# Second attention: probabilities stationary in pieces of 32 queries, in four column tiles of the array, and the result turned by VectorE

## The chip, the core and the metric

The kernel runs on one core of a Trainium2 chip. A core has a matrix engine (TensorE, PE in the profile, its weight loads PEld), VectorE (DVE), ScalarE (ACT), GpSimd (POOL) and SyncE (SP), whose queue issues DMA transfers. They run side by side, each in its own written order, and wait for each other by semaphores. The metric is the device time of one execution in microseconds.

## The reference

Two transformer layers in fp32 over x of 32 x 64 rows of 512. Each layer adds a cross-attention to ctx_4096 and then a feed-forward part: layer 0 has attention over features and a top-2 mixture of 8 experts, layer 1 is this, followed by a gated feed-forward of width 1376:

```python
# second attention: 32 query heads in 8 groups of 4, head dimension 16
q = (layernorm(x) @ Wq).reshape(b, s, 8, 4, 16)
k = (ctx @ Wk).reshape(b, s, 8, 16)
v = (ctx @ Wv).reshape(b, s, 8, 16)
scores = einsum('bqhgd,bkhd->bhgqk', q, k) / 4
attn = softmax(scores, axis=-1)
out = einsum('bhgqk,bkhd->bqhgd', attn, v).reshape(b, s, 512)
x = x + out @ Wo
```

## The kernel before

The program has four phases, one after the other: first attention, experts, second attention (`second_attention`, from line 1021) and feed-forward. The change touches the second attention alone.

That phase works through 16 tiles of 128 rows, two batches of 64 queries each. Within a tile the work goes by batch b (0 or 1) and by g (0 or 1), two of the four heads of every group. `scores` (L1411) multiplies in four row tiles of the array (32 rows each), into the four banks of `ps`; VectorE takes the maximum (L1546) and subtracts it (L1553), ScalarE takes the exponential (L1281), `transpose_probs` (L1435) turns the result on TensorE, `keep_probT` (L1287) copies it to `probT`. `attend(t, b, g)` (L1450) then makes 4 products: stationary is a 128 x 128 block of `probT` (the 64 keys of two key heads by 2 members of the group x 64 queries), moving are 34 columns of `kv` (for two heads 16 values and a column of ones, which gives the softmax's sum). An fp32 product that is no transpose stands in the trace as two pairs of weight load and matmul. After both g, `invert_sums` (L1560) and `keep_attn` (L1565) divide by the sums into `attn`, with the queries on the partitions. `transpose_attn` (L1461) turns `attn` of the whole tile on TensorE, four transposes into bank b2; `keep_high_attn` (L1292, ScalarE) and `keep_low_attn` (L1572, VectorE) split that into a rounded part `aT_hi` and the rest `aT_lo`, and `project` (L1376, L1377, L1381, twelve products of 512 columns) multiplies by Wo. `add_attn` (L1577) adds the result to x.

The order on every engine is written out by hand, one round m of a loop at a time. TensorE in round m: scores(m,0), transpose_x(m+1), attend(m-1,1,0), attend(m-1,1,1), make_q(m+1), scores(m,1), transpose_probs(m,0,0) and (m,0,1), transpose_attn(m-1), attend(m,0,0), transpose_q(m+1), attend(m,0,1), project(m-1), transpose_probs(m,1,0) and (m,1,1). transpose_x(m+1) uses the bank of project and waits for add_attn(m-2) (L1370). VectorE in round m begins with add_attn(m-2) and ends with sum_x2(m+3) (L1519), the norm's sums of a tile three rounds ahead, for which it waits until GpSimd has added the experts' rows to it.

Beside this run three other queues. SyncE in round m: load_x1(m+3) (L1106, from m = 3 on: the ring for x holds 6 tiles, so tiles 6 to 15 are loaded here, each after the store of the tile six before it has landed, L1105), load_kv (L1111), load_gate_up(m+1) (L1117, weights of the feed-forward into one of two stage buffers, after low_part two tiles before), store_x3(m-2) (L1121), store_norm(m-2) (L1125). GpSimd in round m: spread_keys(m+1) (L1205), scale_x2(m+2), add_rows(m+3) (L1177 and L1179), scale_x3(m-2), gather(m+5) (L1168, two indirect DMAs), low_part(m-1) (L1213). ScalarE has, besides the copies and exponentials, high_part(m-1) (L1297), which low_part needs, and norm_x and norm_x3.

Of the kernel before, what the change touches and what calls it, by code (L numbers as in the profile page):

```python
# [13 lines left out]
P = 128  # L14
# [1006 lines left out]
def second_attention(nc, shared, a, late):  # L1021
# [3 lines left out]
    with ExitStack() as stack:  # L1025
# [8 lines left out]
        q_rows, qT, attn, n_out = (sb(n, [P, DIM]) for n in ("q_rows", "qT", "attn", "n_out"))  # L1034
# [4 lines left out]
        smax, rsum = sb("smax", [P, 2, 16]), sb("rsum", [P, 2, 2, KVH, 1])  # L1039
# [8 lines left out]
                 "q_rows_kept qt_made s_shifted exp_done pt_made pt_kept o_made sum_step o_kept at_made ahi_kept alo_kept w_made x3_ready")  # L1048
        (zeroed, const_made, proj_hi_made, proj_lo_made, gu_hi, gu_lo, x2_added, x2_ready, stat_step, mv_ready, rs_step,
         rs_ready, xn_ready, xt_made, xhi_kept, xlo_kept, q_made, q_kept, kv_made, kt_kept, v_kept, keys_ready, s_made, max_step,  # L1050
         q_rows_kept, qt_made, s_shifted, exp_done, pt_made, pt_kept, o_made, sum_step, o_kept, at_made, ahi_kept, alo_kept, w_made, x3_ready,
# [192 lines left out]
        def _(act):  # L1244
# [44 lines left out]
            def keep_high_attn(t):  # L1289
                act.wait_ge(at_made, t + 1)  # L1290
                want(act, w_made, t)
                act.activation(aT_hi[:, :].rearrange("p (g b q) -> p b g q", g=GROUP, b=2),  # L1292
                               b2[:, :].rearrange("p (b g q) -> p b g q", b=2, g=GROUP), ACT.Copy).then_inc(ahi_kept, 1)
# [51 lines left out]
        def _(pe):  # L1345
# [68 lines left out]
            def transpose_probs(t, b, g):  # L1414
                n = 4 * t + 2 * b + g
                pe.wait_ge(exp_done, 2 * t + b + 1)
                if b:
                    if g == 0:
                        want(pe, alo_kept, t)
                        if t == 0:  # L1420
                            pe.wait_ge(q_rows_kept, 2)
                    elif t + 1 < TILES:
                        pe.wait_ge(q_kept, t + 2)
                elif g:
                    if t + 1 < TILES:
                        pe.wait_ge(xlo_kept, t + 2)
                    else:
                        pe.wait_ge(x3_ready, t - 1)
                elif t:
                    pe.wait_ge(pt_kept, 4 * t)  # L1430
                else:
                    pe.wait_ge(q_kept, 1)
                for j in range(4):
                    at = 256 * j + P * g
                    mm = pe.transpose(probs_bank(b, g)[:, P * j:P * j + P], score[:, b, at:at + P], ident[:, :])  # L1435
                mm.then_inc(pt_made, 1)

            def attend(t, b, g):
                n = 4 * t + 2 * b + g
                if n == 0:  # L1440
                    pe.wait_ge(values_zeroed, 3)
                    pe.wait_ge(kt_kept, EARLY)
                    pe.wait_ge(v_kept, EARLY)
                if t >= EARLY and b == 0 and g == 0:
                    pe.wait_ge(kv_loaded[t % 4], 16 * ((t - EARLY) // 4 + 1))
                pe.wait_ge(pt_kept, n + 1)
                want(pe, o_kept, 2 * t + b)
                for j in range(4):
                    at = 136 * g + 34 * j
                    mm = pe.matmul(po[:, at:at + 34], probT[:, g, P * j:P * j + P],  # L1450
                                   kv[:, t % EARLY, P + 136 * b + 34 * j:P + 136 * b + 34 * j + 34], start=True, stop=True)
                mm.then_inc(o_made, 1)

            def transpose_attn(t):
                pe.wait_ge(o_kept, 2 * t + 2)
                if t + 2 < TILES:
                    pe.wait_ge(q_rows_kept, t + 3)
                else:
                    pe.wait_ge(pt_kept, 4 * t + 3)
                for i in range(4):  # L1460
                    mm = pe.transpose(b2[:, P * i:P * i + P], attn[:, P * i:P * i + P], ident[:, :])  # L1461
                mm.then_inc(at_made, 1)
# [19 lines left out]
            for m in range(TILES + 1):  # L1482
# [13 lines left out]
                if 0 <= m - 1 < TILES:  # L1496
                    transpose_attn(m - 1)
# [13 lines left out]
        def _(dve):  # L1511
# [43 lines left out]
            def heads():  # L1555
                return po[:, 0:272].rearrange("p (c h d) -> p c h d", c=2, h=KVH)

            def invert_sums(t, b):
                dve.wait_ge(o_made, 4 * t + 2 * b + 2)
                dve.reciprocal(rsum[:, b, :, :, :], heads()[:, :, :, HD:HD + 1]).then_inc(sum_step, 1)  # L1560

            def keep_attn(t, b):
                dve.wait_ge(sum_step, 2 * t + b + 1)
                want(dve, at_made, t)
                dve.tensor_tensor(attn[:, 256 * b:256 * b + 256].rearrange("p (c h d) -> p c h d", c=2, h=KVH), heads()[:, :, :, 0:HD],  # L1565
                                  rsum[:, b, :, :, :].to_broadcast([P, 2, KVH, HD]), ALU.mult).then_inc(o_kept, 1)

            def keep_low_attn(t):
                dve.wait_ge(ahi_kept, t + 1)
                want(dve, w_made, t)  # L1570
                order = "p (g b q) -> p b g q"
                dve.tensor_tensor(aT_lo[:, :].rearrange(order, g=GROUP, b=2), b2[:, :].rearrange("p (b g q) -> p b g q", b=2, g=GROUP),  # L1572
                                  aT_hi[:, :].bitcast(F32).rearrange(order, g=GROUP, b=2), ALU.subtract).then_inc(alo_kept, 1)
# [33 lines left out]
            for m in range(TILES + 2):  # L1607
# [14 lines left out]
                if 0 <= m - 2 < TILES:  # L1622
                    sum_x3(m - 2)
                    average_x3(m - 2)
# [10 lines left out]
                if m + 3 < TILES:  # L1635
                    sum_x2(m + 3)
                    average_x2(m + 3)
# [368 lines left out]
```

## Time and profile before

| | us |
|---|---|
| Median of 3 runs | 975.94 (974.81 to 982.37) |
| The profiled execution | 983.04, its span 981.3 |
| Granted TensorE clock over the span | 0.955 |
| Second attention in the profiled execution | about 335 to 582 |
| TensorE's work between: attends (L1450), 344 to 560 | 60.0 for 470 records of a matmul |
| transpose_attn (L1461), same stretch | 8.4 for 56 |

The profile counts the time that each engine works; idle time of an engine that does not set the pace costs nothing. A view of the timeline gives the start, the duration and, in brackets, how long the engine stood idle before and what ended that. Records of matmuls overlap, so a group's duration is shorter than the sum of its members.

### The profile page before, as it was taken

Reading aid. Unit: us, or ns where it says so; the run is one execution under the profiler, and the core shown is the slowest. Engines: PE = TensorE matmul, PEld = TensorE weight load, DVE = VectorE, ACT = ScalarE, POOL = GpSimd, SP = SyncE. Lnnn points to the kernel's source line nnn. Section 1 sums busy time; section 2 is a strip of 40 time slices with the busy share of each in tenths; the row PEclk is TensorE's granted clock in tenths of the full one; section 3 lists DMA queues with packets and bytes.
Section 4 is the critical chain, followed back from the end, with each engine's and each line's share of the span. In section 5 each row is a group of like instructions: output and inputs, shape, how many; then the busy total and the mean of one; then the engine's idle time right before and its main releaser. Section 6 shows DMA issues by size and latency. Waiting matters only on the chain. (4 is left out here: it accounts for less than half of the span.)

```text
span 981.3 us, 16773 instructions
## 1 busy us (share of the span) xinstructions
PE 916.7 (93%) x6065; PEld 759.9 (77%) x6065; DVE 435.3 (44%) x866; ACT 348.1 (35%) x567; POOL 293.8 (30%) x415
## 2 busy tenths in 40 slices
PE   6999987899998799999999956999999999999997
PEld 4888876788887688888878845888788788878885
DVE  3988865344444556765657621222312122223112
ACT  3556643233332355555546522222111112111111
POOL 4588863000003665565654220111202000202000
PEclk9999998899998879999989976999999999999999
DMA  8566655794544232434422214111003001202001
GB/s 267 172 226 235 198 188 192 267 312 164 161 149 151 66 105 88 149 104 132 134 80 83 83 54 150 43 43 41 1 11 108 12 0 42 66 1 86 1 1 43
DMA packets 56801, 108.20 MB, mean 110 GB/s; under 512 B 8242, under 2 KB 12338, under 8 KB 56594
## 3 DMA queue, kind: packets, MB, share of 16 engines
q1 hardware_dynamic: 49954, 88.13, 27.8%
q0 software_dynamic: 5120, 16.78, 5.2%
q10 hardware_dynamic: 1648, 2.23, 0.6%
q8 instruction: 51, 0.84, 0.3%
q14 instruction: 28, 0.23, 0.1%
HBM read 67.99 MB, written 39.12 MB: 109 GB/s over the span
## 5 line engine op out<-in xcount | busy, mean ns | idle before, releaser
L1900 DVE SCALAR_TENSOR_TENSOR d_hid<-d_pup,d_b_up,d_silu 128x512 f32<-128x512 f32 (+1 forms) x44 | 33.0, 751 | 235.4 <-PE d_pup L1829 235.4
L1790 ACT ACTIVATE d_silu<-d_pgate,d_b_gate 128x512 f32<-128x512 f32 (+1 forms) x44 | 30.3, 689 | 154.7 <-PE d_pgate L1829 154.7
L1761 POOL TENSOR_TENSOR d_x_res<-d_x_res,d_b_down 128x512 f32<-128x512 f32 x16 | 22.0, 1405 | 187.1 <-DMA d_x_res<-x_after_attention 187.1
L1168 POOL DMA_INDIRECT c_y_in<-expert_results,y_at x32 | 32.7, 1023 | 145.6 <-POOLq L98 137.5
L1827 PE MATMUL d_pgate<-d_nT_hi,gate_up_hi 128*128 128x512 f32 (+1 forms) x176 | 71.5, 406 | 1.4 <-DVE d_nT_lo L1889 1.4
L1797 ACT ACTIVATE d_hid_hi<-d_hid 128x512 fp32r<-128x512 f32 (+1 forms) x44 | 27.8, 632 | 125.3 <-DVE d_hid L1900 125.3
L1829 PE MATMUL d_pgate<-d_nT_hi,gate_up_lo 128*128 128x512 f32 (+1 forms) x176 | 70.3, 400 | 0.0
L1828 PE MATMUL d_pgate<-d_nT_lo,gate_up_hi 128*128 128x512 f32 (+1 forms) x176 | 70.0, 397 | 0.0
L1859 PE MATMUL d_pdown<-d_down_hi,d_hid_hi 128*128 128x512 f32 (+1 forms) x176 | 69.5, 395 | 0.0
L1827 PE MATMUL d_pup<-d_nT_hi,gate_up_hi 128*128 128x512 f32 (+1 forms) x176 | 69.5, 395 | 0.0
L1829 PE MATMUL d_pup<-d_nT_hi,gate_up_lo 128*128 128x512 f32 (+1 forms) x176 | 69.3, 394 | 0.0
L1860 PE MATMUL d_pdown<-d_down_lo,d_hid_hi 128*128 128x512 f32 (+1 forms) x176 | 69.3, 393 | 0.0
L1828 PE MATMUL d_pup<-d_nT_lo,gate_up_hi 128*128 128x512 f32 (+1 forms) x176 | 69.1, 392 | 0.0
L1450 PE MATMUL c_po<-c_kv,c_probT 128*128 128x34 f32 x512 | 66.7, 283 | 0.6 <-ACT c_probT L1287 0.6
L1450 PEld LDWEIGHTS c_po<-c_kv,c_probT 128*128 128x128 f32 x512 | 65.0, 203 | 2.0 <-issue 0.5
L1546 DVE TENSOR_REDUCE c_smax<-c_ps 128x16 f32<-128x1024 f32 x32 | 39.1, 1220 | 38.1 <-PE c_ps L1411 38.1
L1012 DVE TENSOR_TENSOR b_biased<-b_py,b_bias 128x512 f32<-128x512 f32 x39 | 27.0, 691 | 63.8 <-PE b_py L972 63.8
L986 ACT ACTIVATE b_rowsT_hi<-b_pt 128x512 fp32r<-128x512 f32 x39 | 23.4, 600 | 86.3 <-PE b_pt L955 86.3
L1908 DVE TENSOR_TENSOR d_hid_lo<-d_hid,d_hid_hi 128x512 fp32r<-128x512 f32 (+1 forms) x44 | 33.9, 770 | 36.5 <-ACT d_hid_hi L1797 36.5
L1865 PE MATMUL d_pdown<-d_down_hi,d_hid_lo 128*128 128x512 f32 (+1 forms) x176 | 47.8, 393 | 0.0
L1287 ACT ACTIVATE c_probT<-c_bank 128x512 f32<-128x512 f32 x64 | 34.9, 595 | 35.0 <-PE c_bank L1435 35.0
L1281 ACT ACTIVATE c_score<-c_score 128x1024 f32<-128x1024 f32 x32 | 33.7, 1054 | 21.7 <-DVE c_score L1553 21.7
(271 smaller groups left out, 2145.8 us busy)
## 6 DMA issues: line engine op xcount, KB each, us to landing
b_rows<-expert_rows SPq DMA_DIRECT2D x39, 256.0 KB, 2.8
expert_results<-b_result SPq DMA_DIRECT2D x39, 256.0 KB, 2.5
a_wstage<-L_ffn_W_e SPq DMA_DIRECT2D x16, 512.0 KB, 4.2
c_stage<-gate_up SPq DMA_DIRECT2D x16, 344.0 KB, 3.2
late_x<-x_after_attention SPq DMA_DIRECT2D x16, 256.0 KB, 3.8
x_after_attention<-late_x SPq DMA_DIRECT2D x16, 256.0 KB, 3.4
norm_after_attention<-c_n_out SPq DMA_DIRECT2D x16, 256.0 KB, 3.3
d_n_in<-norm_after_attention SPq DMA_DIRECT2D x16, 256.0 KB, 2.8
```

What stands on the lines that cost most here:

```text
L1281: act.activation(score[:, b, :], score[:, b, :], ACT.Exp, scale=SCALE1).then_inc(exp_done, 1)
L1287: act.activation(probT[:, g, :], probs_bank(b, g)[:, :], ACT.Copy).then_inc(pt_kept, 1)
L1450: mm = pe.matmul(po[:, at:at + 34], probT[:, g, P * j:P * j + P], kv[:, t % EARLY, P + 136 * b + 34 * j:P + 136 * b + 34 * j + 34], start= ...
L1546: dve.tensor_reduce(smax[:, b, :].rearrange("p (r g) -> p r g", r=4), all_scores(), AX.X, ALU.max).then_inc(max_step, 1)
L1827: pe.matmul(bank[0:w, :], gu_hi[:, cols], nT_hi[:, g % 2, k, :], start=k == 0, stop=False)
L1828: pe.matmul(bank[0:w, :], gu_hi[:, cols], nT_lo[:, g % 2, k, :], start=False, stop=False)
L1829: mm = pe.matmul(bank[0:w, :], gu_lo[:, cols], nT_hi[:, g % 2, k, :], start=False, stop=k == KD - 1)
L1859: pe.matmul(pdown[n][:, :], hi, down_hi[0:w, i, :], start=i == 0, stop=False)
L1860: pe.matmul(pdown[n][:, :], hi, down_lo[0:w, i, :], start=False, stop=False)
L1865: mm = pe.matmul(pdown[n][:, :], lo, down_hi[0:w, i, :], start=False, stop=i == LAST)
L1900: dve.scalar_tensor_tensor(hid[0:w, s % 2, :], pup[s % 2][0:w, :], b_up[0:w, i:i + 1], silu[0:w, s % 2, :], ALU.add, ALU.mult).then_inc(hi ...
L1908: dve.tensor_tensor(hid_lo[0:w, s % 2, :], hid[0:w, s % 2, :], hid_hi[0:w, s % 2, :].bitcast(F32), ALU.subtract).then_inc(lo_made, 1)
```

## The change

`attend` makes its four products of a 128 x 128 block as sixteen: the stationary side is a piece of 32 queries (128 x 32), and the product of pair of heads j goes to column tile j of the array and so to the partitions 32 j to 32 j + 31 of `po`; the moving side is the same 34 columns. The partitions of `po` now stand for the pair of key heads and a place in a piece, and its columns run over g and q (the piece). `invert_sums` and `keep_attn` treat it in that order. The turned tile comes from a block transpose (32 x 32 blocks) on VectorE, `turn_attn`, two a tile, into a new buffer `attnT` in SBUF; `transpose_attn` on TensorE and its use of bank b2 go. `keep_high_attn` and `keep_low_attn` read `attnT`. transpose_probs(m,1,0), which writes b2, waits for q_rows_kept or pt_kept in place of alo_kept. `turn_attn(m-1, 1)` stands on VectorE between sum_x3 and average_x3, `turn_attn(m, 0)` between sum_x2 and average_x2.

```diff
...
                 act.activation(probT[:, g, :], probs_bank(b, g)[:, :], ACT.Copy).then_inc(pt_kept, 1)
 
             def keep_high_attn(t):
-                act.wait_ge(at_made, t + 1)
+                act.wait_ge(a_turned, 2 * t + 2)
                 want(act, w_made, t)
-                act.activation(aT_hi[:, :].rearrange("p (g b q) -> p b g q", g=GROUP, b=2),
-                               b2[:, :].rearrange("p (b g q) -> p b g q", b=2, g=GROUP), ACT.Copy).then_inc(ahi_kept, 1)
+                act.activation(aT_hi[:, :], attnT[:, :], ACT.Copy).then_inc(ahi_kept, 1)
 
             def high_part(t):
                 act.wait_ge(gu_loaded[t % 2], full(t))
...
                 pe.wait_ge(exp_done, 2 * t + b + 1)
                 if b:
                     if g == 0:
-                        want(pe, alo_kept, t)
-                        if t == 0:
-                            pe.wait_ge(q_rows_kept, 2)
+                        if t + 1 < TILES:
+                            pe.wait_ge(q_rows_kept, t + 2)
+                        else:
+                            pe.wait_ge(pt_kept, 4 * t - 1)
                     elif t + 1 < TILES:
                         pe.wait_ge(q_kept, t + 2)
                 elif g:
...
                     pe.wait_ge(kv_loaded[t % 4], 16 * ((t - EARLY) // 4 + 1))
                 pe.wait_ge(pt_kept, n + 1)
                 want(pe, o_kept, 2 * t + b)
-                for j in range(4):
-                    at = 136 * g + 34 * j
-                    mm = pe.matmul(po[:, at:at + 34], probT[:, g, P * j:P * j + P],
-                                   kv[:, t % EARLY, P + 136 * b + 34 * j:P + 136 * b + 34 * j + 34], start=True, stop=True)
+                for q in range(4):
+                    for j in range(4):
+                        at = 34 * (4 * g + q)
+                        mm = pe.matmul(po[32 * j:32 * j + 32, at:at + 34], probT[:, g, P * j + 32 * q:P * j + 32 * q + 32],
+                                       kv[:, t % EARLY, P + 136 * b + 34 * j:P + 136 * b + 34 * j + 34], start=True, stop=True)
                 mm.then_inc(o_made, 1)
-
-            def transpose_attn(t):
-                pe.wait_ge(o_kept, 2 * t + 2)
-                if t + 2 < TILES:
-                    pe.wait_ge(q_rows_kept, t + 3)
-                else:
-                    pe.wait_ge(pt_kept, 4 * t + 3)
-                for i in range(4):
-                    mm = pe.transpose(b2[:, P * i:P * i + P], attn[:, P * i:P * i + P], ident[:, :])
-                mm.then_inc(at_made, 1)
 
             def project(t):
                 if t == 0:
...
                     scores(m, 1)
                     transpose_probs(m, 0, 0)
                     transpose_probs(m, 0, 1)
-                if 0 <= m - 1 < TILES:
-                    transpose_attn(m - 1)
                 if m < TILES:
                     attend(m, 0, 0)
                 if m + 1 < TILES:
...
                 dve.tensor_tensor(score[:, b, :].rearrange("p (r g e) -> p r g e", r=4, e=64), all_scores(), peak, ALU.subtract).then_inc(s_shifted, 1)
 
             def heads():
-                return po[:, 0:272].rearrange("p (c h d) -> p c h d", c=2, h=KVH)
+                return po[:, 0:272].rearrange("p (n d) -> p n d", d=HD + 1)
 
             def invert_sums(t, b):
                 dve.wait_ge(o_made, 4 * t + 2 * b + 2)
-                dve.reciprocal(rsum[:, b, :, :, :], heads()[:, :, :, HD:HD + 1]).then_inc(sum_step, 1)
+                dve.reciprocal(rsum[:, b, :, :], heads()[:, :, HD:HD + 1]).then_inc(sum_step, 1)
 
             def keep_attn(t, b):
                 dve.wait_ge(sum_step, 2 * t + b + 1)
-                want(dve, at_made, t)
-                dve.tensor_tensor(attn[:, 256 * b:256 * b + 256].rearrange("p (c h d) -> p c h d", c=2, h=KVH), heads()[:, :, :, 0:HD],
-                                  rsum[:, b, :, :, :].to_broadcast([P, 2, KVH, HD]), ALU.mult).then_inc(o_kept, 1)
+                dve.tensor_tensor(attn[:, 256 * b:256 * b + 256].rearrange("p (n d) -> p n d", d=HD), heads()[:, :, 0:HD],
+                                  rsum[:, b, :, :].to_broadcast([P, 16, HD]), ALU.mult).then_inc(o_kept, 1)
+
+            def turn_attn(t, b):
+                dve.wait_ge(o_kept, 2 * t + b + 1)
+                want(dve, ahi_kept, t)
+                want(dve, alo_kept, t)
+                dve.transpose(attnT[:, :].rearrange("p (g b q) -> p b g q", g=GROUP, b=2)[:, b, :, :],
+                              attn[:, 256 * b:256 * b + 256].rearrange("p (g q) -> p g q", g=GROUP)).then_inc(a_turned, 1)
 
             def keep_low_attn(t):
                 dve.wait_ge(ahi_kept, t + 1)
                 want(dve, w_made, t)
-                order = "p (g b q) -> p b g q"
-                dve.tensor_tensor(aT_lo[:, :].rearrange(order, g=GROUP, b=2), b2[:, :].rearrange("p (b g q) -> p b g q", b=2, g=GROUP),
-                                  aT_hi[:, :].bitcast(F32).rearrange(order, g=GROUP, b=2), ALU.subtract).then_inc(alo_kept, 1)
+                dve.tensor_tensor(aT_lo[:, :], attnT[:, :], aT_hi[:, :].bitcast(F32), ALU.subtract).then_inc(alo_kept, 1)
 
             def add_attn(t):
                 dve.wait_ge(w_made, t + 1)
...
                     keep_attn(m - 1, 1)
                 if 0 <= m - 2 < TILES:
                     sum_x3(m - 2)
+                if 0 <= m - 1 < TILES:
+                    turn_attn(m - 1, 1)
+                if 0 <= m - 2 < TILES:
                     average_x3(m - 2)
                 if m < TILES:
                     max_scores(m, 1)
...
                     keep_attn(m, 0)
                 if m + 3 < TILES:
                     sum_x2(m + 3)
+                if m < TILES:
+                    turn_attn(m, 0)
+                if m + 3 < TILES:
                     average_x2(m + 3)
```

## Rows read from the trace of the kernel before

**Rows 1.** The page, part 1: busy time of each engine over the whole execution.
```profile
PE 916.7 (93%) x6065; PEld 759.9 (77%) x6065; DVE 435.3 (44%) x866; ACT 348.1 (35%) x567; POOL 293.8 (30%) x415
```
**Rows 2.** Busy time by stretch: an undisturbed tile, a slowed stretch, the second attention.
```profile
377.00:391.00 14.00, 14.00 (x118) 12.12 (x117) 9.76 (x16) 8.57 (x14) 7.26 (x12) 1.00 0.31 98
500.00:506.00 6.00, 6.00 (x24) 5.13 (x24) 3.39 (x7) 1.44 (x2) 4.41 (x8) 0.54 0.67 184
335.00:582.00 247.00, 235.47 (x1836) 202.00 (x1836) 153.77 (x238) 134.29 (x205) 125.21 (x182) 0.93 0.33 101
```
**Rows 3.** Timeline of one tile: start us, duration us, engine, line, operation.
```profile
377.32 0.76 ACT L1297 ACTIVATE gate_up_hi<-c_stage 128x688 fp32r<-128x688 f32 x1
...
378.17 1.67 POOL L1213 TENSOR_TENSOR gate_up_lo<-c_stage,gate_up_hi 128x688 fp32r<-128x688 f32 x1 [3.27 <-ACT gate_up_hi L1297]
...
380.76 1.87 PE L1450 MATMUL c_po<-c_kv,c_probT 128*128 128x34 f32 x16
...
382.47 0.48 PE L1376 MATMUL c_bank<-c_proj_hi,c_xT_hi 128*128 128x512 f32 x1
...
383.69 0.42 DVE L1565 TENSOR_TENSOR c_attn<-c_po,c_rsum 128x256 f32<-128x256 f32 x1
...
386.09 1.09 PE L1435 MATMUL c_bank<-c_ident,c_score 128*128 128x128 f32 x8
...
386.79 1.08 ACT L1287 ACTIVATE c_probT<-c_bank 128x512 f32<-128x512 f32 x2 [0.65 <-PE c_bank L1435]
...
387.02 0.60 PE L1461 MATMUL c_bank<-c_ident,c_attn 128*128 128x128 f32 x4
...
387.46 1.06 PE L1450 MATMUL c_po<-c_kv,c_probT 128*128 128x34 f32 x8
...
388.35 0.63 PE L1398 MATMUL c_bank<-c_ident,c_q_rows 128*128 128x128 f32 x4
...
388.82 0.98 PE L1450 MATMUL c_po<-c_kv,c_probT 128*128 128x34 f32 x8
...
389.63 0.48 PE L1376 MATMUL c_bank<-c_proj_hi,c_aT_hi 128*128 128x512 f32 x1
...
391.17 0.77 ACT L1297 ACTIVATE gate_up_hi<-c_stage 128x688 fp32r<-128x688 f32 x1
```
**Rows 4.** Timeline around the scores, in row tiles of the array.
```profile
442.58 0.89 PEld L1381 LDWEIGHTS c_bank<-c_proj_hi,c_xT_lo 128*128 128x128 f32 x4
...
442.81 1.09 PE L1381 MATMUL c_bank<-c_proj_hi,c_xT_lo 128*128 128x512 f32 x4
...
443.84 0.73 PE L1411 MATMUL c_ps<-c_keys,c_qT 32*128 32x128 f32 x16
...
444.49 1.09 PE L1435 MATMUL c_bank<-c_ident,c_score 128*128 128x128 f32 x8
```
**Rows 5.** First attention, 64x64 tiles: timeline; then by line (busy us, mean ns).
```profile
107.13 1.15 PE L542 MATMUL a_po<-a_v,a_probT 64*64 64x65 f32 x32
...
L542 PE MATMUL a_po<-a_v,a_probT 64*64 64x65 f32 x512 | 19.2, 226 | 1.0 <-ACT a_probT L438 1.0
```
**Rows 6.** Timeline of GpSimd and of SyncE's queue, one turn of their loop.
```profile
424.10 1.69 POOL L1213 TENSOR_TENSOR gate_up_lo<-c_stage,gate_up_hi 128x688 fp32r<-128x688 f32 x1
...
432.81 1.29 POOL L1177 TENSOR_TENSOR late_x<-late_x,c_y_in 128x512 f32<-128x512 f32 x1 [4.97 <-DMA late_x<-x_after_attention]
...
439.30 1.67 POOL L1213 TENSOR_TENSOR gate_up_lo<-c_stage,gate_up_hi 128x688 fp32r<-128x688 f32 x1
...
426.20 0.42 SPq L1121 DMA_DIRECT2D x_after_attention<-late_x  x1
...
430.05 0.32 SPq L1106 DMA_DIRECT2D late_x<-x_after_attention  x1
```
**Rows 7.** Timeline: TensorE's longest wait, and the loop's last turn.
```profile
499.12 0.63 PE L1370 MATMUL c_bank<-c_ident,c_xn 128*128 128x128 f32 x4 [2.15 <-DVE late_x L1577]
...
514.00 1.66 POOL L1213 TENSOR_TENSOR gate_up_lo<-c_stage,gate_up_hi 128x688 fp32r<-128x688 f32 x1 [0.36 <-ACT gate_up_hi L1297]
```

More of the change, by code:

```diff
@@ L1033, in second_attention @@
         xn = sb("xn", [P, 2, DIM])
-        q_rows, qT, attn, n_out = (sb(n, [P, DIM]) for n in ("q_rows", "qT", "attn", "n_out"))
+        q_rows, qT, attn, attnT, n_out = (sb(n, [P, DIM]) for n in ("q_rows", "qT", "attn", "attnT", "n_out"))
         y_in = sb("y_in", [P, 4, DIM])
@@ L1038, in second_attention @@
         score, probT = sb("score", [P, 2, 1024]), sb("probT", [P, 2, DIM])
-        smax, rsum = sb("smax", [P, 2, 16]), sb("rsum", [P, 2, 2, KVH, 1])
+        smax, rsum = sb("smax", [P, 2, 16]), sb("rsum", [P, 2, 16, 1])
         stats, mv, rstd = sb("stats", [P, 2, 6]), sb("mv", [P, 2, 2]), sb("rstd", [P, 2, 2])
@@ L1047, in second_attention @@
                  "rs_ready xn_ready xt_made xhi_kept xlo_kept q_made q_kept kv_made kt_kept v_kept keys_ready s_made max_step "
-                 "q_rows_kept qt_made s_shifted exp_done pt_made pt_kept o_made sum_step o_kept at_made ahi_kept alo_kept w_made x3_ready")
+                 "q_rows_kept qt_made s_shifted exp_done pt_made pt_kept o_made sum_step o_kept a_turned ahi_kept alo_kept w_made x3_ready")
         (zeroed, const_made, proj_hi_made, proj_lo_made, gu_hi, gu_lo, x2_added, x2_ready, stat_step, mv_ready, rs_step,
          rs_ready, xn_ready, xt_made, xhi_kept, xlo_kept, q_made, q_kept, kv_made, kt_kept, v_kept, keys_ready, s_made, max_step,
-         q_rows_kept, qt_made, s_shifted, exp_done, pt_made, pt_kept, o_made, sum_step, o_kept, at_made, ahi_kept, alo_kept, w_made, x3_ready,
+         q_rows_kept, qt_made, s_shifted, exp_done, pt_made, pt_kept, o_made, sum_step, o_kept, a_turned, ahi_kept, alo_kept, w_made, x3_ready,
          ) = (sem(n) for n in names.split())
```

## The prediction

> **What bounds the kernel now.** I read the busy times of the page first, then the busy time by stretch, the timeline of one tile of the second attention on every engine, and last the waits of that stretch, followed through GpSimd and SyncE's queue. TensorE is busy 93% of the span [rows 1], 235.47 us of 247 in the second attention [rows 2]; the change touches nothing outside that stretch. But a busy TensorE is not yet the bound. In an undisturbed tile it works all 14 of 14 us with VectorE at 9.76 [rows 2], and one tile follows the other after 13.85 us (high_part at 377.32 and at 391.17) [rows 3]. Sixteen such tiles are 222 us; the stretch takes 247. The rest is a second clock: low_part on GpSimd (424.10, 1.69 us) frees a stage buffer, only then does SyncE's queue get past load_gate_up and issue store_x3 (426.20), the next load of x1 waits for that store to land (430.05), its rows land at 432.81 after GpSimd has waited 4.97 us, two additions, the norm's scalars and two gathers follow, and low_part comes again at 439.30 [rows 6]. That is 15.2 us, 1.35 us more than TensorE's tile, with no instruction of the attention in it. From low_part at 378.17 to that at 514.00 there are nine turns, 15.1 us each [rows 3, 7]. TensorE catches up with this loop and then waits: sum_x2 waits for the added rows at the head of VectorE's queue, add_attn and the bank for transpose_x behind it, 2.15 us at 499.12 [rows 7]. A clock granted at half (0.54 in the mean of 500 to 506) follows that wait [rows 2]. At both ends of the loop low_part waits for ScalarE instead (3.27 us before 378.17, 0.36 before 514.00) [rows 3, 7]: there TensorE sets the pace.
>
> **Attend.** An attend is now 8 pairs of weight load and matmul (4 products, each in two passes), 0.89 us (387.46 to 388.35) [rows 3], so 0.112 us a pair. The moving side is 34 columns; what costs is the load of 128 columns. The change makes it 32 pairs, each loading 32 columns, with four column tiles in turn. What a pair costs there no row shows. The nearest: the scores, four row tiles, loads of 128 columns, 16 pairs from 443.84 to 444.49, 0.041 us a pair with both switches of tiling in it [rows 4]; and 64x64 tiles, loads of 64 columns, 32 pairs in 1.15 us, 0.036 us each [rows 5]. If each of the two diagonal tiles in use takes a pair in turn, that is 16 rounds of (1.15 - 0.23) / 16 = 0.058 us (0.23 is the record of the last one, which runs out after its start). 0.112 us for 128 columns and 0.058 for 64 lie on one line that gives 0.031 for 32. Both ends: four tiles fully at once are 8 rounds of 0.031, 0.25 us an attend; one pair after another at 0.031 is 1.0 us, and at the 64x64 rows' price as measured 32 x 0.036 = 1.15 us. I take 0.30 us, near the lower end, since the scores are the nearest row in kind: 128-column loads that alone take 0.112 pass there at 0.041 or less, so tiles do load beside each other.
>
> **Switching the tiling.** The scores' 16 pairs, four at a time, would be 4 x 0.112 = 0.45 us. The product ahead of them streams its last 512 columns until about 443.75 (last start 442.81 + 1.09 - 0.39 = 443.51, and 0.23 from one product to the next), and the transposes start at 444.49 [rows 4]: 0.74 us, so in and out cost 0.3 us, 0.15 each. Now attends need no switch; after the change three blocks of a tile do: the two attends of the tile before (A), and each of the two first attends by itself (B, C), because transpose_q stands between them.
>
> **One tile, step by step** [rows 3]. A: 380.76 to 382.47, 1.71 us, becomes 2 x 0.30 + 0.3 = 0.9: 0.8 us saved. B and C: transpose_attn goes (4 transposes, 387.02 to 387.46), but the attend behind it needs probT, which ScalarE begins to copy at 386.79, 0.54 us each, so B starts at 387.4 or later with or without the transposes: that removal buys a wait of 0.4 us and is worth nothing. From 387.46 to 389.63, 2.17 us, becomes 0.30 + 0.15 + 0.47 (transpose_q) + 0.15 + 0.30 + 0.15 = 1.5: 0.7 saved. Together 1.5 us a tile, 13.85 to 12.35.
>
> **VectorE and ScalarE.** Added: two block transposes of 128x256 a tile. Nearest row: the product 128x256, 0.42 us [rows 3]; ends: 0.25 (a reciprocal-sized minimum) and four times the row, 1.7, if 4-byte elements went in pieces. I take 0.4, so 0.8 us a tile; VectorE goes to about 10.6 of 12.35 us. The one of b=1 stands ahead of max_scores(m,1), whose scores come later than VectorE; the one of b=0 stands behind sum_x2, so in the loop it waits for the rows of x, and its reader (keep_high_attn, one iteration later) has time. The copy and the subtraction of the turned tile read SBUF instead of PSUM, same count and size: nothing. No DMA is added or moved, none of SyncE's or GpSimd's instructions.
>
> **The sum.** 16 x 1.5 = 24 us is what TensorE saves, not what the kernel saves. Between 378.17 and 514.00 the loop keeps its 15.1 us, and a faster TensorE waits there instead. What counts: two tiles before 378.17, 3.0 us, which also bring the loop forward; and after 514.00 tiles 12 to 15 and the drain, about 4.3 tiles, 6.5 us. 9.5 in all. Against it: TensorE now stands some 2.8 us in each turn, more than the 2.15 that a half clock followed; in the loop that hides in the same slack, but the last turn hands it on (6 us at about half clock cost 3 us of work; half of that, 1.5). Forecast: 8 us less. The profiled execution took 983.04 us (span 981.3), 7 above the median of three, 975.94, so 975 against it and **968** against the median.
>
> **Rivals.**
> (1) Pairs one after another. Column tiles share all 128 rows, the row tiles of the scores and the diagonal 64x64 tiles share none, so no row shows two loads into the same rows at once. At 0.031 a pair an attend takes 1.0 us: A 2.3 instead of 1.71, B and C 2.9 instead of 2.17, 1.3 us a tile lost, 15.15 us a tile, just the loop's turn: 6.3 x 1.3 = 8 us, **984**; up to 16 x 1.3 = 21, 997, if half clocks eat the slack. It decides from 0.67 us an attend on (0.021 a pair), where 4 attends and 0.75 of switches (B's way in hides behind its wait) equal today's 1.71 + 2.17 - 0.47 = 3.41 us. The Trainium skill, page "TensorE: Matmul & The Clock Gate", Part 3, has a rule on this side: a weight load overlaps matmuls in flight only when its row group differs. The trace agrees in part only: the load at 442.58 to 443.47 runs beside products of the same rows from 442.81 [rows 4], so one load ahead is overlapped; several are not shown. The same section gives 2.38 times for three column tiles, at 512 moving columns, which speaks for the forecast; no run here shows that.
> (2) The loop is not rigid, or the undisturbed runs hardly meet it: then all 16 tiles count, 24 us, **952**. Against it: nine turns in a row at 15.1 us.
> (3) Loads come four at once but are fed too slowly (64 instructions an attend for 16): 0.5 to 0.67 us an attend, 0 to 0.7 us a tile: **971 to 976**, no change that can be told.
> (4) A column-tiled load costs like a full one (0.112 a pair, 3.6 us an attend), or a block transpose at the fourfold price binds VectorE: from 10 us slower up; the former 16 x 9 = 150 us.
>
> **Chances.** Forecast 0.45; (3) 0.17; (1) 0.23; (2) 0.08; (4) 0.07. Within the forecast 0.25 to 0.40 us an attend and 0 to 3 us of half clock give 962 to 973. The range: 959, between the forecast's low end and (2), to 989, which takes in (1) at its own price and some of its half clocks; out are most of (2), the worst of (1), and (4), about 2 in 10. About 1% (9.8 us) is what a measurement can tell from no change: faster than 966.2 is a third of the forecast and all of (2), 0.25; slower than 985.7 is half of (1) and (4), 0.19; the rest, 0.56, is the same.
>
> **What would show it.** In the changed kernel's timeline: an attend of 32 pairs in about 0.3 us (1.0 is rival 1); 0.3 us around each block; attend(m,0,0) starting no earlier after the probabilities' transposes than now; VectorE's block transposes near 0.4 us; tiles 12 to 15 at about 12.4 us apart; low_part still about 15.1 us apart between its second and its eleventh; TensorE's wait for add_attn in every turn of the loop, 2 to 3 us each, where it is now one of 2.15 us here and there; a half clock after them. The forecast is wrong if an attend takes over 0.67 us, or if the loop's turn shortens with TensorE's tile.

## The result, and the profile after

The changed kernel took 971.2 us (median of 20 runs, 965.29 to 979.04) against 979.38 us for the kernel before in the same comparison (20 runs, 974.45 to 988.4): 8.2 us less, a ratio of 0.9908 with a 95% interval of 0.9885 to 0.993. The forecast was 8 us less, and 968 us counted from the median of three runs, 975.94; the twenty runs put the kernel before 3.4 us higher, so the absolute time came out 3.2 us above the forecast. The profiled execution after has a span of 968.6 us, 12.7 less than the one before.

Part 1 of the page after, to be set against [rows 1]:

```profile
PE 878.3 (91%) x7537; PEld 710.9 (73%) x7537; DVE 439.0 (45%) x898; ACT 350.1 (36%) x567; POOL 295.6 (31%) x415
```

TensorE works 38 us less, and the span is shorter by a third of that. The busy times by stretch (length, then PE, PEld, DVE, ACT and POOL with their counts, granted clock, DMA share, GB/s) answer to [rows 2]: a tile near the end, a slowed stretch, the whole second attention.

```profile
537.00:549.00 12.00, 11.62 (x208) 9.10 (x207) 9.42 (x15) 7.75 (x12) 3.78 (x7) 1.00 0.26 75
496.00:502.00 6.00, 4.80 (x75) 3.82 (x76) 4.72 (x9) 2.21 (x3) 5.33 (x8) 0.68 0.51 120
333.00:568.00 235.00, 202.69 (x3308) 156.95 (x3308) 161.13 (x269) 136.15 (x205) 127.34 (x183) 0.95 0.35 107
```

TensorE now stands for 32 us of its stretch, where it stood for 11.5. The timeline of the tile near the end, in the kernel after, beside [rows 3]:

```profile
539.03 0.77 PE L1451 MATMUL c_po<-c_kv,c_probT 128*32 128x34 f32 x64
539.88 0.47 PE L1375 MATMUL c_bank<-c_proj_hi,c_xT_hi 128*128 128x512 f32 x1
...
542.80 0.43 DVE L1560 STREAM_TRANSPOSE c_attnT<-c_attn 128x256 f32<-128x256 f32 x1
...
543.50 1.09 PE L1435 MATMUL c_bank<-c_ident,c_score 128*128 128x128 f32 x8
...
544.89 0.46 PE L1451 MATMUL c_po<-c_kv,c_probT 128*32 128x34 f32 x32 [0.30 <-issue]
545.17 0.63 ACT L1292 ACTIVATE c_aT_hi<-c_attnT 128x512 fp32r<-128x512 f32 x1
545.28 0.66 PE L1397 MATMUL c_bank<-c_ident,c_q_rows 128*128 128x128 f32 x4
545.87 0.46 PE L1451 MATMUL c_po<-c_kv,c_probT 128*32 128x34 f32 x32
...
546.26 0.51 PE L1375 MATMUL c_bank<-c_proj_hi,c_aT_hi 128*128 128x512 f32 x1
```

Two attends with the way out take 0.85 us (539.03 to 539.88), one with its way out 0.39 (544.89 to 545.28). Not every attend of this execution is so short: between 348 and 498 us 11 of the 64 take 0.8 to 1.9 us, with idle stretches inside; the last experiment comes back to them. The groups of lines over the second attention (busy us, mean ns of one, idle before):

```profile
L1451 PE MATMUL c_po<-c_kv,c_probT 128*32 128x34 f32 x2048 | 32.7, 200 | 12.7 <-issue 10.3 <-ACT c_probT L1287 2.3
...
L1560 DVE STREAM_TRANSPOSE c_attnT<-c_attn 128x256 f32<-128x256 f32 x32 | 13.8, 430 | 0.1
```

The loop is still there. GpSimd and SyncE's queue in the kernel after, one turn, beside [rows 6]:

```profile
403.92 1.68 POOL L1213 TENSOR_TENSOR gate_up_lo<-c_stage,gate_up_hi 128x688 fp32r<-128x688 f32 x1
...
406.01 0.42 SPq L1121 DMA_DIRECT2D x_after_attention<-late_x  x1
...
409.56 0.32 SPq L1106 DMA_DIRECT2D late_x<-x_after_attention  x1
...
413.37 1.28 POOL L1177 TENSOR_TENSOR late_x<-late_x,c_y_in 128x512 f32<-128x512 f32 x1 [5.72 <-DMA late_x<-x_after_attention]
...
419.83 1.67 POOL L1213 TENSOR_TENSOR gate_up_lo<-c_stage,gate_up_hi 128x688 fp32r<-128x688 f32 x1
```

And its second and eleventh low_part, with TensorE's longest wait between them, beside [rows 7]:

```profile
373.58 1.65 POOL L1213 TENSOR_TENSOR gate_up_lo<-c_stage,gate_up_hi 128x688 fp32r<-128x688 f32 x1 [3.17 <-ACT gate_up_hi L1296]
...
496.23 0.63 PE L1369 MATMUL c_bank<-c_ident,c_xn 128*128 128x128 f32 x4 [2.87 <-DVE late_x L1570]
...
511.04 1.65 POOL L1213 TENSOR_TENSOR gate_up_lo<-c_stage,gate_up_hi 128x688 fp32r<-128x688 f32 x1
```

Nine turns took 137.5 us where they had taken 135.8 (514.00 - 378.17). The difference of the two profiled executions, counted from scores(0,0) (335.2 before, 333.3 after) to the last add_attn (580.81 and 567.70), is 11.2 us: 2.7 less up to the second low_part, 1.6 more in the nine turns, 10.1 less behind the eleventh.

The first of these terms lies near the forecast's 3.0 by luck, since each execution lost about 3 us there: the one before to a half clock,

```profile
346.00:358.00 12.00, 11.84 (x64) 9.95 (x68) 6.21 (x10) 3.91 (x7) 10.30 (x12) 0.57 0.36 115
```

the one after to three of the long attends. From scores(0,0) to the second low_part they took 43.0 and 40.3 us; two kernels with the old attends measured below take 39.8 there, the changed kernel traced once more and with its stores first 37.3. That is 2.5 us without these disturbances.

In the last term there is a half clock too. The drain of the execution before, and then that of the kernel after:

```profile
562.00:581.00 19.00, 16.94 (x78) 14.25 (x76) 6.55 (x12) 7.27 (x11) 4.65 (x8) 0.73 0.11 43
```
```profile
550.00:568.00 18.00, 12.11 (x266) 9.31 (x264) 11.46 (x22) 9.89 (x15) 4.95 (x8) 1.00 0.32 109
```

19 us at a mean of 0.73 are about 5.1 us lost, an estimate that counts all of it as work. It would leave 5.0 us saved there, and 6 in the stage. But the half clock is not peculiar to this one execution. The kernel before with the stores first, below, has it again at the same place:

```profile
548.00:567.00 19.00, 16.93 (x78) 14.33 (x76) 6.53 (x12) 7.26 (x11) 4.63 (x8) 0.74 0.13 49
```

The variants of the changed kernel have 3 to 10 us of it there, and only the two traces of the changed kernel itself have none. So how much of the 10.1 us is work saved and how much is clock stays open.

### The profile page after: what moved, and what is told of

The parts are those of the page before. It is cut to its first block and busy times, and to the rows that moved or that the text cites. A ratio compares the mean times of both kernels' runs of the same rounds, so it can differ in the third digit from the quotient of the medians.

```text
span 968.6 us, 19733 instructions
## 1 busy us (share of the span) xinstructions
PE 878.3 (91%) x7537; PEld 710.9 (73%) x7537; DVE 439.0 (45%) x898; ACT 350.1 (36%) x567; POOL 295.6 (31%) x415
## 5 line engine op out<-in xcount | busy, mean ns | idle before, releaser
L1907 DVE TENSOR_TENSOR d_hid_lo<-d_hid,d_hid_hi 128x512 fp32r<-128x512 f32 (+1 forms) x44 | 31.5, 715 | 36.2 <-ACT d_hid_hi L1796 36.2
L1451 PE MATMUL c_po<-c_kv,c_probT 128*32 128x34 f32 x2048 | 32.7, 200 | 12.7 <-issue 10.3
L1451 PEld LDWEIGHTS c_po<-c_kv,c_probT 128*32 128x32 f32 x2048 | 25.2, 110 | 24.0 <-issue 19.5
```

Of the source, the lines that this page charges most:

```text
L1451: mm = pe.matmul(po[32 * j:32 * j + 32, at:at + 34], probT[:, g, P * j + 32 * q:P * j + 32 * q + 32], kv[:, t % EARLY, P + 136 * b + 34 * ...
```

## The experiments

Kernels that share a median of the kernel before (976.94, 978.98 or 976.17) ran in one comparison with it.

**The loop taken off TensorE, under both kernels.** In SyncE's rounds the two stores go ahead of the load that waits for low_part; nothing else changes.

```diff
-                if 0 <= m - 1 and m + 1 < TILES:
-                    load_gate_up(m + 1)
                 if 0 <= m - 2 < TILES:
                     store_x3(m - 2)
                     store_norm(m - 2)
+                if 0 <= m - 1 and m + 1 < TILES:
+                    load_gate_up(m + 1)
```

In the changed kernel:

> The changed kernel, with SyncE's queue in another order: in each round store_x3 and store_norm are issued ahead of load_gate_up instead of behind it, so the next load of x1 no longer waits, after low_part, for a store to land (3.9 us of the loop's 15.2). Theory L, that the loop of low_part, store, load, additions and gathers held the time: the loop's turn falls to about 11.3 us, TensorE's tile of 12.4 us sets the pace, and the nine turns of 15.3 us become 12.4: about 25 us less than the changed kernel, 945 to 950 us, and TensorE's waits for add_attn go from 10 us to under 2. Rival R, that the saved TensorE work was worth only 8 us because the tile itself did not get shorter, and that the order of the stores has nothing to do with it: 971 us, no change.

Measured: 947.6 us (943.7 to 951.7), ratio to the kernel before (976.94) 0.9691 [0.965, 0.9731]. In the kernel before:

> The kernel before, with the same reordering of SyncE's queue and nothing else. Theory L: the nine turns of 15.1 us become TensorE's own 13.85, 11 us less, and some 2 to 4 us of half clocks behind the waits go too: 964 to 968 us. The distance to the changed kernel with the same reordering is then what the column tiles are worth when nothing hides them, 16 tiles of 1.3 to 1.5 us, 20 to 24 us, in place of the 8 measured. Rival R: no change, 979 us, and the distance stays 8 us.

Measured: 968.12 us (962.27 to 970.91), ratio 0.9896 [0.9858, 0.9934]. So the change is worth 20.5 us where the loop hides less of it, and 8.2 where it hides most. Stretches of 370 to 500, the kernel before with the stores first and then the changed kernel with the stores first:

```profile
370.00:500.00 130.00, 130.00 (x1082) 112.83 (x1081) 90.58 (x142) 80.31 (x124) 81.03 (x118) 1.00 0.41 128
```
```profile
370.00:500.00 130.00, 122.00 (x2083) 95.37 (x2081) 100.86 (x171) 85.97 (x131) 87.85 (x125) 0.99 0.46 137
```

With 128-column attends TensorE is now the only limit in this stretch: its tiles are 13.9 us apart throughout. With the column tiles it still stands 8 of 130 us: it waits for add_attn for 4.9 us in six places of the stage, where under 2 were expected. The longest of these waits, in one turn of that kernel's loop:

```profile
429.02 1.69 POOL L1213 TENSOR_TENSOR gate_up_lo<-c_stage,gate_up_hi 128x688 fp32r<-128x688 f32 x1
...
430.73 0.33 SPq L1117 DMA_DIRECT2D c_stage<-gate_up  x1
431.17 0.37 SPq L1106 DMA_DIRECT2D late_x<-x_after_attention  x1
...
437.23 1.28 POOL L1177 TENSOR_TENSOR late_x<-late_x,c_y_in 128x512 f32<-128x512 f32 x1 [4.48 <-DMA late_x<-x_after_attention]
...
441.71 1.08 PE L1369 MATMUL c_bank<-c_ident,c_xn 128*128 128x128 f32 x4 [2.28 <-DVE late_x L1570]
...
443.69 1.67 POOL L1213 TENSOR_TENSOR gate_up_lo<-c_stage,gate_up_hi 128x688 fp32r<-128x688 f32 x1
```

The store is out of the way, but the load of x still stands behind the load of weights, which waits for low_part. This turn takes 14.7 us; the eight from the second low_part on take 12.2 to 15.1, 13.5 in the mean.

**What a pair costs when its tile is not left.** The changed kernel with the stores first, the two loops of `attend` exchanged, so that eight pairs in a row go to one column tile:

```diff
-                for q in range(4):
-                    for j in range(4):
+                for j in range(4):
+                    for q in range(4):
```

> The changed kernel with the stores first, and in attend the two loops exchanged: j outside, q inside, so that four products in a row (eight pairs) go to the same column tile. Same products, same addresses. Theory T, that an attend costs 0.28 us because four column tiles load and multiply beside each other while each takes its pairs one after another at 0.031 us: now they come one after another, 32 x 0.031 = 1.0 us an attend (as priced in rival 1), 2.8 us more a tile, 35 to 45 us slower than the kernel with the stores first. Rival: the short loads alone give the gain and the order of the tiles does not matter: 0.3 us an attend and no change.

Measured: 963.29 us (960.42 to 969.12), 15.7 us more than with the tiles in turn, where 35 to 45 were expected. A part of its timeline:

```profile
437.12 0.91 PE L1451 MATMUL c_po<-c_kv,c_probT 128*32 128x34 f32 x32 [0.25 <-ACT c_probT L1287]
437.95 0.66 PE L1397 MATMUL c_bank<-c_ident,c_q_rows 128*128 128x128 f32 x4
438.54 0.91 PE L1451 MATMUL c_po<-c_kv,c_probT 128*32 128x34 f32 x32
```

An attend with its way out takes 0.83 us instead of 0.39. In the single records the pairs of one tile start 0.030 us apart, as the line through 0.112 and 0.058 had it, but the next tile's first pairs start before the eight of the former are through (one tile from 430.67, the next from 430.83, 0.16 and not 0.24 apart). That gives some 0.7 us from the first start to the last, not 1.0: a tile of 13.8 us against 12.3, or 24 us in 16 of them. The measured 15.7 are 8 less; the faster kernel still waits at the loop, and this one has no wait for add_attn, which explains the direction but was not measured apart. So the gain does rest on tiles that work at once, and the price of rival 1, taken over into this expectation, was 0.3 us an attend too high, because neighbouring tiles overlap even there.

**The two first attends next to each other**, which spares one switch in and one out. The changed kernel with the stores first:

```diff
                     attend(m, 0, 0)
+                    attend(m, 0, 1)
                 if m + 1 < TILES:
                     transpose_q(m + 1)
-                if m < TILES:
-                    attend(m, 0, 1)
```

> The changed kernel with the stores first, and on TensorE transpose_q(m+1) behind attend(m,0,1) instead of between the two attends, so that B and C are one block in column tiles. Theory W (block C then waits for ScalarE's second copy of probabilities, which ends 1.09 us after the first began, so the switch saved is waited for): at most 0.1 us a tile, within 2 us of the kernel with the stores first. Rival: each way in and out costs its 0.3 us on the path: 0.3 us a tile, 5 us faster. A loss is possible if keep_q, now later on ScalarE, delays the exponential of b=1.

Measured: 944.78 us (943.0 to 948.62), ratio 0.9682 [0.9643, 0.9722], 2.8 less than with the stores first alone, with overlapping ranges. Its timeline, then that of the stores first alone:

```profile
429.28 1.08 ACT L1287 ACTIVATE c_probT<-c_bank 128x512 f32<-128x512 f32 x2 [0.65 <-PE c_bank L1435]
...
429.93 0.95 PE L1451 MATMUL c_po<-c_kv,c_probT 128*32 128x34 f32 x64 [0.25 <-ACT c_probT L1287]
430.81 0.66 PE L1397 MATMUL c_bank<-c_ident,c_q_rows 128*128 128x128 f32 x4
431.22 0.48 PE L1375 MATMUL c_bank<-c_proj_hi,c_aT_hi 128*128 128x512 f32 x1
```
```profile
433.46 0.46 PE L1451 MATMUL c_po<-c_kv,c_probT 128*32 128x34 f32 x32 [0.25 <-ACT c_probT L1287]
433.85 0.66 PE L1397 MATMUL c_bank<-c_ident,c_q_rows 128*128 128x128 f32 x4
434.44 0.46 PE L1451 MATMUL c_po<-c_kv,c_probT 128*32 128x34 f32 x32
434.83 0.50 PE L1375 MATMUL c_bank<-c_proj_hi,c_aT_hi 128*128 128x512 f32 x1
```

1.29 us against 1.37: putting them together is worth 0.1 us a tile, not 0.3, as theory W had it. The two attends take 0.88 us where one takes 0.39, because the second waits for ScalarE's second copy: in the single records that copy ends at 430.37 and the second attend starts at 430.42, just as the first starts at 429.93 behind the first copy's end at 429.88. So the switch that is spared is waited for, and this run does not give its price. Where both copies are there, as in the block at 539.03 of the kernel after, the second attend follows without a pause.

**The terms that were set at nothing.** The changed kernel with the stores first, once more as the yardstick:

> The changed kernel with the stores first once more, so that the next three are compared with it in the same rounds: 947 us, within 3.

Measured: 946.96 us (944.8 to 948.74), kernel before 978.98. Beside it the same with each block transpose done a second time into a buffer that nobody reads:

```diff
+                dve.transpose(spare[:, :].rearrange("p (g b q) -> p b g q", g=GROUP, b=2)[:, b, :, :],
+                              attn[:, 256 * b:256 * b + 256].rearrange("p (g q) -> p g q", g=GROUP)).then_inc(spare_made, 1)
```

> The changed kernel with the stores first, and each block transpose on VectorE done a second time into a spare buffer that nobody reads, right behind the first: 32 more of 0.43 us, 0.86 us a tile. Theory S (VectorE works about 10.3 of 12.4 us, and both block transposes stand where VectorE is ahead of what follows): at most 0.3 us a tile, 0 to 4 us slower than with the stores first; TensorE's tile stays at 12.3 us where nothing waits. Rival: VectorE is by now as much the bound as TensorE, and 0.86 us a tile shows whole, 14 us.

Measured: 948.73 us (947.68 to 950.64), 1.8 more, with overlapping ranges. And with the four transposes of attn on TensorE put back ahead of attend(m,0,0), their result unread:

```diff
+                if 0 <= m - 1 < TILES:
+                    transpose_attn(m - 1)
                 if m < TILES:
                     attend(m, 0, 0)
```

> The changed kernel with the stores first, and TensorE's four transposes of attn done again at their old place ahead of attend(m,0,0), into bank b2, whose content nobody reads: 64 transposes, 0.44 us a tile. Theory W (attend(m,0,0) waits for ScalarE's copy of the probabilities anyway, so taking the transposes out was worth nothing): attend(m,0,0) starts no later than without them, 0 to 1.5 us in all. Rival: the transposes' 0.44 us are on the path and half of what the change gave per tile: 7 us slower.

Measured: 947.84 us (945.92 to 949.68), 0.9 more, within the spread. The timeline of this last kernel:

```profile
439.94 1.09 PE L1436 MATMUL c_bank<-c_ident,c_score 128*128 128x128 f32 x8
...
440.87 0.60 PE L1463 MATMUL c_bank<-c_ident,c_attn 128*128 128x128 f32 x4
441.40 0.46 PE L1452 MATMUL c_po<-c_kv,c_probT 128*32 128x34 f32 x32
```

The attend starts 1.46 us after the transposes of the probabilities, and 1.34 with nothing between (432.12 to 433.46): the four transposes lie under ScalarE's copy but for 0.1 us. The tiles that wait for nothing say the same: 12.3 us with the stores first, 12.3 with the second block transpose, 12.4 with the transposes put back. Both terms stood rightly at about nothing.

**The loop opened altogether.** The load of weights goes back to its old place behind the load of kv, but one round later, so that it no longer stands ahead of a load of x that could go; here with the attends next to each other:

```diff
+                if 2 <= m < TILES:
+                    load_gate_up(m)
                 if 0 <= m - 2 < TILES:
                     store_x3(m - 2)
                     store_norm(m - 2)
-                if 0 <= m - 1 and m + 1 < TILES:
-                    load_gate_up(m + 1)
```

> The changed kernel with the two attends adjacent, and SyncE's queue with load_gate_up one round later (load_gate_up(m) instead of (m+1), at its old place behind load_kv and ahead of the stores), so that low_part, which it waits for, was over a round before: low_part is out of the loop, and the next load of x1 is issued as soon as the norm of the tile before is stored. Theory L: TensorE's remaining waits for add_attn (about 4.5 us and the half clocks) go, tiles of 12.2 us throughout, 3 to 7 us less than with the two attends adjacent alone: 938 to 942 us. Rival: the remaining waits come from the transfers beside each other, not from the order; then 944 us stays.

Measured: 940.89 us (936.53 to 944.7), ratio 0.961 [0.9574, 0.9646], the lowest median of all kernels here. Then without the exchange of the attends, and in the kernel before:

> The changed kernel with load_gate_up(m) behind load_kv and ahead of the stores, one round later, and the attends where the change has them. Theory L: tiles of 12.3 us throughout, 942 to 945 us, so the two first attends next to each other account for 1 to 3 of the 6 us between 946.9 and 940.9. Rival (the six came from the neighbouring attends through the clock): 946 to 948.

> The kernel before, with load_gate_up(m) issued behind load_kv and ahead of the stores, one round later than there: the SyncE queue then never waits for low_part ahead of a store. Theory L (the loop of stores, loads and GpSimd was the only limit beside TensorE, and at the tile of the kernel before the exchange of the stores already cleared it): same as with the stores issued first, 966 to 970 us, tiles of 13.9 throughout, no wait of transpose_x for add_attn. Rival (the loop still cost something behind the exchange, in the runs that were not profiled): 958 to 963 us.

Measured: 941.8 us (938.21 to 945.48), ratio 0.9658 [0.9619, 0.9697], and 967.34 us (964.74 to 973.38), ratio 0.9933 [0.9905, 0.9962], both against 976.17. Their difference is 25.5 us: the whole of what the column tiles save on TensorE, 16 tiles of 13.9 us made 16 of 12.3. How the 6 us from 946.96 to 940.89 part between the loop and the neighbouring attends is not shown. By the medians the loop has 5.2 and the attends 0.9, but the two kernels ran in different comparisons; by the ratios (0.9681, 0.9658, 0.961) it is 2 and 5, each within some 4 us. The tiles are 12.3 us apart in one and 12.2 in the other. The stretch of 370 to 500 in the kernel of 940.89 us:

```profile
370.00:500.00 130.00, 126.01 (x2258) 99.51 (x2257) 110.00 (x181) 91.35 (x141) 95.58 (x135) 1.00 0.46 138
```

**The changed kernel once more, for its trace.**

> The changed kernel once more, for its trace. If the idle stretches of 0.4 to 0.5 us in and ahead of attends, put down to issue (10.3 us in 26 places), belong to the kernel, they come again at the same attends and in about that sum; if they belong to that execution, the sum is under 3 us as in the kernels with the stores first. Either way tiles between the second and the eleventh low_part come 15 to 15.5 us apart, the time is 965 to 977 us, and transpose_x waits for add_attn in about every second turn, with a half clock behind the longer waits.

Measured: 960.79 us in its one run, below the 965 to 977 expected. The same two attends in the execution profiled first, and in this one:

```profile
388.15 0.75 PE L1451 MATMUL c_po<-c_kv,c_probT 128*32 128x34 f32 x31
...
389.36 0.52 PE L1451 MATMUL c_po<-c_kv,c_probT 128*32 128x34 f32 x33 [0.46 <-issue]
```
```profile
385.62 0.77 PE L1451 MATMUL c_po<-c_kv,c_probT 128*32 128x34 f32 x64
```

What each waited for between 345 and 500 (us in all, times, longest), the first execution and then this one:

```profile
PE c_po L1451 <- issue: 8.8, 21, 0.5
```
```profile
PE c_bank L1369 <- DVE late_x L1570: 12.7, 7, 2.8
...
PE c_po L1451 <- issue: 1.2, 4, 0.3
```

So the idle stretches inside the attends belong to an execution, not to the kernel. Without them TensorE meets the loop and waits for add_attn in seven tiles of that stretch, 1.8 us each. Nine turns of the loop take 132.2 us here (370.92 to 503.14), where the first execution took 137.5 and the kernel before 135.8; from scores(0,0) to the last add_attn the stage takes 224.5 us against 234.4. One pair of profiled executions can thus not prove the single terms of an 8 us difference.

## Why the prediction was right, step by step

- **Attend.** Forecast 0.30 us, ends 0.25 and 1.15. The single records show groups of four starts, 6 to 7 ns apart at first, a group every 0.03 to 0.04 us, 0.26 us from the first start to the last: the lower end, four tiles fully at once. 53 of the 64 attends of the first trace take 0.26 to 0.30 us. The other 11 take 0.8 to 1.9, over the 0.67 that was named as the sign of being wrong; in the second trace none takes over 0.49, so they are not the price of an attend. The rule quoted from the Trainium skill, page "TensorE: Matmul & The Clock Gate", Part 3, that a load overlaps only matmuls of another row group, does not hold here: these tiles share all 128 rows, and 32 pairs of load and matmul pass in 0.26 us, where one after another, at the 0.030 us of a pair in one tile, they would take about 0.96 (an estimate). The section's 2.38 times for three column tiles was not measured. Eight pairs in a row in one tile cost 0.44 us more an attend than tiles in turn.
- **Switching.** Forecast 0.15 in and 0.15 out. Out: 0.14 us behind the last group of a single attend. In: transpose_q's four (545.28, 0.11 us each) to the next attend at 545.87 leave 0.15. The run with the attends adjacent does not test these prices, since its second attend waits for ScalarE. Block A takes 0.85 us (0.9 forecast), B and C 1.37 (1.5): saved 1.6 us a tile, forecast 1.5.
- **transpose_attn worth nothing, VectorE's transposes covered.** B starts 1.39 us behind the probabilities' transposes (543.50 to 544.89), before 1.37 (386.09 to 387.46). A block transpose takes 0.43 us, forecast 0.4. Both were confirmed by putting the work back: +0.9 and +1.8 us, inside the ranges.
- **The loop.** The step that carried the forecast, and it held to within half a microsecond a turn: nine turns of 15.1 us before, 15.3 after, 14.7 in the second trace. Two orders of SyncE's queue that loosen it raise the change's worth from 8.2 to 20.5 and 25.5 us. What stood out in the profile before was a busy TensorE; what decided was a chain without one instruction of the attention in it.
- **The ends.** Before the loop 2.7 us were saved in the profiled pair and 2.5 where nothing disturbs (3.0 forecast). Behind it 10.1 us, where 6.5 less 1.5 were forecast; up to 5.1 of them may be the half clock in the drain of the kernel before, which neither trace of the changed kernel has. The forecast had no term for it. That 8 was forecast and 8.2 measured is thus partly luck: this term, the 1.6 us more or 3.6 us less in the loop, and the runs' spread of 14 us are each as large as what the single terms are off.
- **Waits for add_attn in every turn, 2 to 3 us, a half clock behind them.** Only half right. In the first trace there were six with 10.0 us in all. Three half clocks lie behind them (about 419 to 427, 450 to 458 and 498 to 505 us), with 18.7, 17.9 and 19.4 us between two scores(m,0), otherwise 12.3 to 14.8; the two turns of the loop without a wait follow the first two of these tiles, whose lost work had used up the slack. In the second trace there were nine with 15.7 us in all, nearly every turn, but 1.7 us each.
- **The rivals.** Rival 1 fell by the 0.26 us; its mechanism is real, but comes only if the tiles are not taken in turn, and costs 0.7 us an attend. Rival 2, that all tiles count, is what the kernel does once the loop is opened (24 us forecast, 25.5 measured). Rival 3, loads fed too slowly, could not be told from the forecast by the time: 971.2 us lies in its 971 to 976 as well as in the forecast's 962 to 973. It fell by the 0.26 us and by the second trace; the idle stretches of the first look like it, but their cause is open. Rival 4 fell by the attend and the block transpose (its 16 x 9 was too small a sum: 4 x 3.6 + 0.75 - 3.41 is 11.7 us a tile; nothing hangs on it).

Open: what makes the idle stretches of 0.4 to 0.5 us in the attends. The changed kernel issues 64 instructions where 16 stood, and its trace has 62 packets of instruction fetch; but the place of the fetches did not match the stretches, and no run was made on that. Open too is how much of the 971 us belongs to such stretches: the execution without them was 9.5 us shorter in its span, but it is a single run of another comparison.

## What to carry to other kernels

Before costing an edit of the busiest engine, measure the distance between repetitions of every other queue's instruction: here low_part came every 15.1 us and TensorE's own tile took 13.85, so two thirds of the 25 us saved were waited away. When a saving vanishes so, look in the DMA queue for a transfer that waits in front of others which could go; moving one load by a round here raised the worth of the change from 8 to 25 us. The products with few moving columns went by the columns of their stationary side here (0.112 us a pair for 128, about 0.058 for 64, 0.030 for 32, with 34 or 65 moving), so narrow column tiles were cheap once consecutive instructions went to different tiles. And take a second trace before reading small terms out of one: two executions of the same kernel differed here by 9.9 us in one stage.

## What the runs showed of the hardware

- Column tiles that share all rows load and multiply at once: 32 pairs (128 x 32 stationary, 34 moving columns, fp32) in 0.26 us, one after another in the same tile 0.030 us a pair.
- Two attends next to each other take 0.85 us with their way out if both copies of the probabilities are there (539.03 to 539.88; the 64 starts lie within 0.57 us), one takes 0.39. The 0.24 us between the last group of one attend and the next in the run with the attends adjacent (430.181 to 430.421) are a wait for ScalarE's copy.
- A granted clock at half (the lower of the two levels, 1.2 instead of 2.4 GHz) came with some of TensorE's waits in the loop: 6.8 us from 498.1 behind the 2.87 us before 496.23, 3.4 us from 441.2, within the 2.28 us before 441.71. It did not come with all: the changed kernel's second trace has the full clock from 500 to 510 us, around a wait of 2.53 us before 503.71, and the kernel before has 0.54 over 562 to 573 us with no wait above 0.8 us in the ten before. The kernel with the loop opened, which had no wait for add_attn, had the full clock between 353 and 527 us.
- A block transpose of 128 x 256 fp32 on VectorE takes 0.43 us, as much as a product of that size; read from SBUF the turned tile costs ScalarE 0.63 us, where PSUM cost 0.60.
